# Written-out gathers without staged indices, and a four-piece VectorE add, in a graph network on one core

## What is computed

```python
src, dst = (edge_index[0], edge_index[1])
msg = jax.nn.relu(x[src] + edge_attr)                       # 21250 x 512
agg = jax.ops.segment_sum(msg, dst, num_segments=x.shape[0])
h = x + agg
h = jax.nn.relu(h @ W1 + b1) @ W2 + b2
h = x + h
mean = h.mean(axis=0); var = h.var(axis=0)
h = (h - mean) * jax.lax.rsqrt(var + BN_EPS) * gamma + beta
```

## Time and profile before

| | us |
|---|---|
| runs | 764.68 median of 3 (764.16 to 765.23) |
| profiled execution: span from its first to its last instruction | 770.4 |
| PE busy | 635.7 (83%) |
| DVE (VectorE) busy | 397.7 (52%) |
| POOL busy | 383.3 (50%) |
| ACT (ScalarE) busy | 262.4 (34%) |

### The profile page before, as it was taken

The page is one execution under the profiler, slowest core; times in us unless marked ns, Lnnn a source line. Parts: engine busy times, 40 slices in busy tenths (PEclk is TensorE's granted clock), DMA queues, the critical chain, the costliest instruction groups (busy, mean ns, idle before and its releaser), DMA issues.

```text
span 770.4 us, 9550 instructions
## 1 busy us (share of the span) xinstructions
PE 635.7 (83%) x2854; PEld 411.5 (53%) x2854; DVE 397.7 (52%) x765; ACT 262.4 (34%) x434; POOL 383.3 (50%) x401
## 2 busy tenths in 40 slices
PE   2597886998988988999886877988898978798963
PEld 1343335997888827988521333433354433345962
DVE  3798882766648492117443333434443434432767
ACT  1354442112463154111532423244333332343135
POOL 7388888201012038300177777777776777760000
PEclk9699997999999998999899899998999989999985
DMA  7600000000002000024568788877888788650003
GB/s 225 183 2 0 1 0 4 0 0 1 1 1 94 17 1 1 0 71 162 192 234 272 251 309 290 280 267 272 311 297 307 253 284 279 207 149 0 1 0 134
DMA packets 30332, 103.09 MB, mean 134 GB/s; under 512 B 6559, under 2 KB 7201, under 8 KB 24986
## 3 DMA queue, kind: packets, MB, share of 16 engines
q1 hardware_dynamic: 16858, 58.59, 21.4%
q0 software_dynamic: 13440, 44.05, 18.0%
HBM read 97.51 MB, written 5.12 MB: 133 GB/s over the span
## 4 chain that ended last, share of the span: by engine, by line
PE 33%; POOL 31%; issue 17%; DVE 9%; ACT 5%; DMA 3%; POOLq 1%; ACTq 0%; SPq 0%; DVEq 0%
POOL xg L471 25%; PE ps L1171 15%; PE ps L1196 8%; PE ps L1369 3%; POOL hot_lo L395 3%; POOL idx L467 2%; DVE stats L871 2%; DVE xn L891 2%; ACT countsT L563 2%; PE ps L1131 1%; DMA xg<-x_dram,idx 1%; PE ps L1146 1%; DMA row_src_i<-in_src_dram 1%; PE ps L1332 1%; PE ps L1311 1%
## 5 line engine op out<-in xcount | busy, mean ns | idle before, releaser
L471 POOL DMA_INDIRECT xg<-x_dram,idx x168 | 217.3, 1293 | 73.4 <-issue 40.2
L1311 PE MATMUL ps<-ea,hot_w 128*38 128x512 f32 x336 | 170.2, 654 | 50.6 <-ACT ea L636 50.5
L978 DVE TENSOR_TENSOR ea<-ea,xg 128x2048 f32<-128x2048 f32 x42 | 96.3, 2292 | 180.6 <-DMA xg<-x_dram,idx 180.6
L636 ACT ACTIVATE ea<-ea 128x2048 f32<-128x2048 f32 x42 | 80.2, 1910 | 186.9 <-DVE ea L978 186.9
L1311 PEld LDWEIGHTS ps<-ea,hot_w 128*38 128x38 f32 x336 | 38.3, 124 | 151.4 <-issue 95.2
L395 POOL TENSOR_SCALAR hot_lo<-iota_n,lo_col 128x128 bf16<-128x128 f16 x84 | 56.5, 683 | 8.6 <-POOL lo_col L391 8.6
L1131 PE MATMUL ps<-hot_code,hot_lo 128*128 128x380 bf16 x168 | 38.1, 353 | 20.3 <-POOL hot_lo L395 20.2
L777 DVE TENSOR_SCALAR hot_code<-iota_n,codeT 128x380 bf16<-128x380 f16 x168 | 52.6, 373 | 4.2 <-issue 3.8
L1332 PE MATMUL ps<-zg,w_s 128*128 128x114 f32 x448 | 53.6, 278 | 0.4 <-ACT zg L652 0.4
L467 POOL COPY idx<-srcT_i 128x4 int32 (+1 forms) x42 | 19.2, 456 | 66.9 <-issue 66.7
L1332 PEld LDWEIGHTS ps<-zg,w_s 128*128 128x128 f32 x448 | 51.1, 192 | 1.1 <-ACT zg L652 0.5
(11 more groups left out here) (193 smaller groups left out, 1092.7 us busy)
## 6 DMA issues: line engine op xcount, KB each, us to landing
ea<-in_edge_attr_dram SPq DMA_DIRECT2D x41, 1024.0 KB, 6.9
w_s<-in_L_gnn_W_dram SPq DMA_DIRECT2D x5, 1024.0 KB, 11.6
xg<-x_dram,idx POOLq DMA_INDIRECT x168, 5.3
xn<-in_x_dram SPq DMA_DIRECT2D x3, 768.0 KB, 13.1
x_dram<-xn SPq DMA_DIRECT2D x9, 256.0 KB
out_dram<-xn SPq DMA_DIRECT2D x9, 256.0 KB
w_s<-in_L_gnn_W_dram SPq DMA_DIRECT2D x2, 512.0 KB, 9.0
b_b<-in_L_gnn_b_dram SPq DMA_DIRECT2D x3, 256.0 KB, 5.6
```

What stands on the lines that cost most here:

```text
L471: pool.indirect_dma_start(out=xg[:, slot, r, :], out_offset=None, in_=x3_dram[:, :], in_offset=bass.IndirectOffsetOnAxis(ap=idx4[:, slot, ...
L636: act.activation(ea[:, s, :, :], ea[:, s, :, :], ACT.Relu).then_inc(relu_done, 1)
L978: dve.tensor_tensor(ea[:, s, :, :], ea[:, s, :, :], xg[:, slot, :, :], ALU.add).then_inc(add_done, 1)
L1311: ins = pe.matmul(ps[0:W, 4 + s % 2, :], hot_w[:, s, r, :], ea[:, s, r, :], start=(r == 0), stop=(r == TPG - 1))
```

## The change

The gathers of all 42 groups are written out on POOL, so that the group number is a constant and each indirect DMA takes its indices from `srcT_i` itself; the copy into `idx4`, its wait and its count are gone, and so is the loop. POOL waits once more for `idx_ready` ahead of the stream. On VectorE the add of 128 x 2048 becomes four adds of 128 x 512, and the last of them counts `add_done`.

```diff
+            pool.wait_ge(idx_ready, 1)
             pool.wait_ge(x3_stored, 16 * NT)
...
-            def gather(it, s):
-                g, slot = RING * it + s, s % XRING
-                if not (isinstance(g, int) and g < XRING):
+            def gather(g):
+                slot = g % XRING
+                if g >= XRING:
                     pool.wait_ge(add_done, g - XRING + 1)
-                pool.tensor_copy(idx4[:, slot, :], srcT_i[:, bass.ds(g, 1), :].rearrange("p a b -> p (a b)")).then_inc(idx_staged, 1)
-                pool.wait_ge(idx_staged, g + 1)
-                pool.sem_inc(idx_seen, 1)
                 for r in range(TPG):
                     pool.indirect_dma_start(out=xg[:, slot, r, :], out_offset=None, in_=x3_dram[:, :],
-                                            in_offset=bass.IndirectOffsetOnAxis(ap=idx4[:, slot, r:r + 1], axis=0)).then_inc(xg_loaded[slot], 16)
-
-            for s in range(RING):
-                gather(0, s)
-            with pool.Fori(1, ITERS) as it:
-                for s in range(RING):
-                    gather(it, s)
+                                            in_offset=bass.IndirectOffsetOnAxis(ap=srcT_i[:, g, r:r + 1], axis=0)).then_inc(xg_loaded[slot], 16)
+
+            for g in range(NG):
+                gather(g)
...
-                dve.tensor_tensor(ea[:, s, :, :], ea[:, s, :, :], xg[:, slot, :, :], ALU.add).then_inc(add_done, 1)
+                for r in range(TPG):
+                    ins = dve.tensor_tensor(ea[:, s, r, :], ea[:, s, r, :], xg[:, slot, r, :], ALU.add)
+                ins.then_inc(add_done, 1)
```

More of the change, by code:

```diff
@@ L265, in gnn_kernel @@
         xg_loaded = [sem(f"xg_loaded{i}") for i in range(XRING)]
-        idx_staged, idx_seen = sem("idx_staged"), sem("idx_seen")
+        idx_seen = sem("idx_seen")
         add_done, relu_done, win_ready = sem("add_done"), sem("relu_done"), sem("win_ready")
```

## The result

The changed kernel takes **707.8 us** in the median of four runs (707.1 to 709.2); the kernel before takes 764.4 beside it (764.2 to 765.2). The ratio is 0.927 (0.923 to 0.930), 56.6 us less: 5 us more than forecast, and inside the range. The profiled execution after took 708.0 us with a span of 706.3, against a span of 770.4 before. In the runs on record a span is about 1.7 us shorter than its execution's time (1.6 to 1.8), so the execution profiled before took about 772.1, 7.7 above the median of its runs, and this one 0.2 above its own. That is why the spans differ by 64.1: 7.5 us of it are not the change. The gain didn't show in every later comparison: in one of them this same kernel was no faster than the one before, which is told further down.

What follows compares the result with a forecast made beforehand. The prediction took POOL to pace every group at 7.36 us. Saving 41.8 us over 36 groups at 6.2 and 9.6 over the first six, 51.4 together, turned the median 764.7 into 713 us, range 699 to 740.

Steps and rivals of the forecast that it cites:

- POOL set the pace before: In the stream, POOL's 5.70 us of issue plus 1.64 of stretching make 7.34, explaining the 7.36 a group.
- its 0.70: On POOL, dropping the index copy and its wait cuts a group's issue from 5.70 to 5.00 us.
- The catch: A POOL gather that comes inside a VectorE add waits for its end: 1.64 us a group, 0.7 with four pieces.
- no way in: Rival: gathers cannot enter between add pieces, so POOL waits for the last; 6.9 us a group, 745 us, chance 0.10.
- the prediction's 0.12: On POOL, the us added after a gather's 0.30 lead to time when it comes for its index.
- The pieces: On VectorE, each 512-column add takes about 0.69 us, four back to back 2.5 against 2.29 for the whole add.
- Lock-step: Rival: VectorE and POOL wait for each other at every piece; POOL 7.44 us a group, 768 us, slower, chance 0.03.
- the 6.2 us a group for the 36 groups: Pace assumed for groups with block parts and joins, down from 7.36, saving 41.8 us.
- all three floors: Per group in the stream: POOL 5.7 us, TensorE 5.87 to 6.04, DMA 5.8 to 6.2.
- The extrapolated 336 GB/s: DMA rate at 100% busy, from 262 GB/s at 78%; it gives 6.24 us a group.
- the rival of a DMA that gives less: Rival: bunched requests make gathers land late, 6.75 us a group, 733 us; chance 0.15 for 724 to 740.
- The first six groups: Almost no joins there, so POOL's 5.7 us holds; 6 x 1.6 = 9.6 us saved.

Runs made afterwards that it cites:

- the gathers alone: Kernel before with gathers written out without the index copy, VectorE's add still one instruction of 2048 columns: 731.3 us, ratio 0.960.
- the adds alone: Kernel before, loop and index copy kept, its add split into four of 512 columns: 723.8 us, ratio 0.950.
- written out with the copy: Kernel before with all 42 gathers written out, index copy and whole add kept: 765.5 us, ratio 1.004.
- half the join: Half of the join's matmuls left out: in the kernel before 761.4 us; in the changed kernel 738.8 us, then 686.3 in another comparison.
- later reloads: Changed kernel with SP reloading a place of `ea` two groups later: 767.4 us, then 765.2 (ratio 1.000) on another chip.
- the two pieces: Changed kernel with two adds of 1024 columns instead of four of 512: 712.9 us, ratio 0.934.
- the comparison on the other chip: Beside the kernel before (764.4 us): changed kernel unchanged 708.6, with half the join 686.3, with scatter turned by using `ea` as weights 747.7.
- The first four experiments: Run side by side: gathers alone 731.3 us, adds alone 723.8, written out with the copy 765.5, changed kernel with two adds 712.9.

## Why the prediction was right, and where it was off

**POOL set the pace before: right.** The sum of issue and stretching met the period in three more kernels: 6.42 and 6.42 with the gathers alone, 6.20 and (643.0 - 3 x 0.61 - 388.0) / 41 = 6.18 with the adds alone, 7.23 and 7.26 written out with the copy. The copy gone is worth its 0.70, and the 0.30 taken ahead of a group's first gather stood.

**The catch: right in kind, too large in size.** Gathers come in between the pieces, against the rival of no way in (745). Four pieces cost 0.50 a group in the kernel before, against 0.7 forecast. In the changed kernel the stretching is (169.8 - 168 x 0.946) / 42 = 0.26, and 2.06 of its 10.9 us are one gather caught by a whole instruction ahead of the stream, which is why the maximum is still 3009 ns and not 1.6 us. POOL and VectorE at one add:

```profile
397.68 1.41 POOL L469 DMA_INDIRECT xg<-x_dram,srcT_i  x1 [0.30 <-issue]
399.39 0.95 POOL L469 DMA_INDIRECT xg<-x_dram,srcT_i  x1 [0.30 <-issue]
...
397.58 2.54 DVE L974 TENSOR_TENSOR ea<-ea,xg 128x512 f32<-128x512 f32 x4 [2.06 <-DMA xg<-x_dram,srcT_i]
```

The caught gather ends at 399.09, 0.82 after the end of the first piece (397.58 + 0.69 = 398.27), as forecast. The next is not caught: by the prediction's 0.12 it reaches for its index at 399.51, just as the piece running then ends. The steps are 1.24 and 2 x 0.61 = 1.22, equal within what the rows tell; the prediction priced that meeting as a second catch of up to 0.57. What a clear margin would do wasn't tried.

**The pieces: right.** 685 ns at the median against 0.69 forecast, four in 2.54 against 2.5.

**Lock-step (768): refuted.** The longest of 168 pieces took 737 ns, 52 above the median. The Trainium skill (SBUF — State Buffer, section "SBUF: two separate sides") lets whichever starts first hold the shared ports for its whole instruction while the other fully blocks. The gathers behind an add agree; the adds behind a gather don't.

**The mis-sized term is the 6.2 us a group for the 36 groups.** It was 5.87. I had put it above all three floors because each would sometimes miss, and at what 262 GB/s extrapolates to. With the rings six and three deep none missed: TensorE has no gap in 200 us. 36 x 0.33 = 11.9 too little, less 1.6 because those groups took 7.31 and not 7.36 before, is the 10.3 by which 52.1 exceeds 41.8. The extrapolated 336 GB/s was too low as well: 353 over 200 us, 397 over 24 us, with both kinds in flight. The Trainium skill (HBM Reference, section "Specifications (TRN2)") says that a core streaming alone measures well above its share of about 358 GB/s; the 397 agree, while the 353 come from a stretch that TensorE paces. So the rival of a DMA that gives less (733) fell too.

**The first six groups: 9.6 forecast, 8.2 measured.** POOL's 5.7 was not their bound alone; TensorE waits 5.10 us for the fourth group, and that scatter then runs slowly, 5.84.

**The closeness is in part luck.** In spans the forecast of 51.4 was 12.7 short of 64.1: 10.3 from the 36 groups and 3.9 from the earlier start, less 1.4 from the first six. In medians it was only 5.2 short of 56.6, because the 7.36 us a group came from an execution 7.7 us slower than the median, which the prediction carried over to the median as if it were part of the saving. Other traces of kernels that POOL paces with copy and whole add have 7.26 (written out) and (688.1 - 391.7) / 41 = 7.23 (half the join).

**What no rival held:** that TensorE's counts can come so late that a kernel paced by TensorE loses the gain. It showed in all four traces of such kernels in two of the later comparisons (the kernel itself, half the join, later reloads twice), and in none of the first result, of the two pieces, and of the comparison on the other chip. The kernels paced by POOL did not slow beside them (761.4 and 763.4 us in the one, 763.9 in the other). The first four experiments and the set that was disturbed ran on the same chip, so the chip alone doesn't decide it. What holds the counts back isn't settled, and neither is why POOL-paced kernels escape. One rival was not tested: that TensorE's own supply of instructions stalls, for which its stops inside joins would speak.

No kernel tried that computes the whole result was shown to beat the changed one.

## What to carry to other kernels

When POOL issues gathers beside long two-input VectorE instructions, add up POOL's own time at the undisturbed duration; the excess of the mean over the median is what cutting the VectorE instruction can return, here 1.64 us down to 0.50, and two pieces may do. When a bound is removed, the next floor, summed from rows without gaps, is the best estimate for a kernel with deep rings, not a value some per cent above it. And cost a shorter sequence of narrow matmuls at both clock levels before trusting its instruction times. Last, measure a gain again beside the kernel before in a second comparison: this one stood in two comparisons and was absent in a third, for a cause that stays open.

## What the hardware showed unexpectedly

- **Late counts.** The same program took 708 us in two comparisons and 766 in another. In the slow one, counts of TensorE reached ScalarE and SP up to 20.8 and 15.8 us after the modelled end of the matmuls at the first long stop, and TensorE stopped inside joins for about 1.7 us at a time.
- **A lower clock without idle time.** With 38-column matmuls the granted clock was 0.76 over 180 us in which no TensorE row ends before the next begins; with the 512-column scatters it was 1.00 in the same window, on the same chip.
- **DMA beyond the extrapolation.** 397 GB/s at a share of 1.01 with gathers and loads mixed, while the landings grew only by 1.2 and 1.1 us.
- **One-sided catching.** A gather inside an add waits for its end; in the changed kernel's trace a 512-column add never grew by more than 52 ns beside 168 gathers.
